# A four-stage image network on one core: softplus of the small pass earlier, gate later, sums moved, more banks in the small scans

## The reference

```
x = x + mamba_pyramid(gn(x))     # block 0, touched by the change
x = x + attention(gn(x))         # block 1, 8 heads of 32, 1024 tokens
x = x + dilated_depthwise(gn(x)) # block 2
x = x + attention_ln(gn(x))      # block 3
```

```
delta = softplus(dt(f) + dtb); dA = exp(delta * A); dBx = delta * B * f
h = h * dA + dBx               # along the tokens, 128 channels x 16 states
y = sum_n(h * C) + f * D; y = layernorm(y)
```

## Time and profile before

| | |
|---|---|
| median of 3 runs (range) | 5007.52 us (5001.81 to 5014.78) |
| profiled execution: time, span | 5008.71 us, 5007.0 us |
| mean granted clock of PE | 0.876 |
| busy: PE, DVE, ACT, POOL | 82%, 71%, 43%, 44% |
| from one sample's output to the next's | 617 to 624 us |
| of it in the 48 scans (sample 1) | 162 us |

### The profile page before, as it was taken

One profiled execution on the slowest core, in us unless ns is written; L12 is line 12 of the kernel. 1 busy time (PEld: TensorE's weight loads), 2 busy tenths in 40 slices (PEclk: granted clock), 3 DMA queues, 4 the chain that ended last, 5 costly groups with the idle time before them and its releaser, 6 DMA issues. The chain is left out here.

```text
span 5007.0 us, 46959 instructions
## 1 busy us (share of the span) xinstructions
PE 4130.5 (82%) x17450; PEld 1976.1 (39%) x17450; DVE 3559.5 (71%) x4904; ACT 2164.6 (43%) x2623; POOL 2205.8 (44%) x777
## 2 busy tenths in 40 slices
PE   5699976999769997699976999769896798967988
PEld 2254432444324443244433444334443344423443
DVE  6865787657776577765777757877678675786756
ACT  4334453335533355243552435524355242652525
POOL 4731546315464155540555505555056450564505
PEclk8799987999879997799977999779997799977999
DMA  1020200201002110021100210002200012001120
GB/s 39 0 60 1 51 9 0 60 16 36 9 0 60 22 31 9 1 60 28 24 9 9 52 36 16 9 9 52 48 4 9 21 40 51 1 9 26 27 51 10
DMA packets 62967, 125.92 MB, mean 25 GB/s; under 512 B 18825, under 2 KB 21001, under 8 KB 62482
## 3 DMA queue, kind: packets, MB, share of 16 engines
q1 hardware_dynamic: 62738, 122.91, 10.6%
HBM read 12.23 MB, written 8.39 MB: 4 GB/s over the span
## 5 line engine op out<-in xcount | busy, mean ns | idle before, releaser
L1039 DVE TENSOR_REDUCE mx<-PS 128x1 f32<-128x512 f32 x2048 | 1280.0, 684 | 418.2 <-PE PS L1407 416.9
L675 ACT ACTIVATE PT<-PS 128x1024 f32<-128x1024 f32 x1024 | 999.9, 1021 | 856.6 <-PE PS L1512 847.4
L430 POOL TENSOR_TENSOR piece<-PT 128x2048 f32<-128x2048 f32 x48 | 220.2, 4588 | 1890.5 <-ACT PT L675 1890.5
L1407 PE MATMUL PS<-KS,QS 96*128 96x512 f32 x2048 | 841.4, 470 | 66.8 <-DVE mx L1039 29.4
L430 POOL TENSOR_TENSOR piece<-piece,PT 128x2048 f32<-128x2048 f32 x192 | 880.1, 4584 | 16.4 <-ACT PT L675 1.5
L1512 PE MATMUL PS<-QS,KS 98*128 98x512 f32 x2048 | 670.4, 419 | 41.2 <-DMA QS<-nm 41.0
L410 POOL TENSOR_TENSOR work<-work,Crep 128x1024 f32<-128x1024 f32 x256 | 605.0, 2392 | 57.6 <-PE PS L1287 37.1
L1407 PEld LDWEIGHTS PS<-KS,QS 96*128 96x128 f32 x2048 | 374.5, 197 | 566.7 <-DVE mx L1039 401.3
L1460 PE MATMUL PS<-PT,Vt 128*32 128x512 f32 x4096 | 548.1, 607 | 26.5 <-DVE oT L1063 19.3
L1327 PE MATMUL PS<-dstk,sel 128*128 128x512 f32 (+1 forms) x640 | 292.5, 529 | 230.9 <-DVE work L924 93.7
L1512 PEld LDWEIGHTS PS<-QS,KS 98*128 98x128 f32 x2048 | 382.2, 197 | 247.2 <-ACT PT L675 110.8
(11 more groups left out here) (222 smaller groups left out, 5359.8 us busy)
## 6 DMA issues: line engine op xcount, KB each, us to landing
QS<-piece SPq DMA_DIRECT2D x384, 128.0 KB, 2.4
KS<-piece SPq DMA_DIRECT2D x384, 128.0 KB, 2.4
xin<-x SPq DMA_DIRECT2D x8, 1024.0 KB
out<-xr SPq DMA_DIRECT2D x8, 1024.0 KB, 4.0
W<-wpack SPq DMA_DIRECT2D x2, 1024.0 KB
QS<-nm SPq DMA_DIRECT2D x128, 8.0 KB, 1.9
W<-wpack SPq DMA_DIRECT2D x1, 576.0 KB
W<-wpack SPq DMA_DIRECT2D x2, 256.0 KB
```

The costliest lines, as they stand in the source:

```text
L430: pool.tensor_tensor(total, first, PT[:, i % PT_RING, :, :], ALU.add).then_inc(sum_pool.sem, 1)
L675: act.activation(PT[:, i % PT_RING, 2 * pr:2 * pr + 2, :], PS[:, 2 + 2 * pr:4 + 2 * pr, :], ACT.Exp, scale=SCALE).then_inc(p_sb.sem, 1)
L1039: dve.tensor_reduce(mx[:, at, cc:cc + 1], PS[:, row_slot(n, cc), :], AX.X, ALU.max).then_inc(r_max.sem, 1)
L1407: pe.matmul(PS[:, row_slot(n, cc), :], QS[0:kd, c, h, q * P:q * P + P], KS[0:kd, h, cc * N:cc * N + N], start=True, stop=True).then_inc(r_ ...
```

## The change

Six edits, all in block 0 but the last:

1. The small pass's softplus input (`coeff(2, 0, Wd)`) is computed earlier on PE, and ACT runs its softplus right after `head_of_input(0)`, ahead of the coefficient copies of pass 1.
2. The gate moves: its two halves go to banks 1 and 0, the first ahead of the scans, the second on PE after n = 1, and ACT applies Silu (two halves, both table loads) ahead of its work for n = 2.
3. The ring of C products gets eight slots (two of them in `xr`), and most sums go at 4q + 8 instead of 4q + 6.
4. The inputs of states 19 and 31 are made by DVE and no longer by ACT and POOL.
5. In the small scans u goes to banks 2 and 3 in turn and d to banks 4, 6, 5, 7 in turn; the waits follow.
6. In attention the head of the negative maximum is copied as soon as it is there, the rest by ACT's queue; at the first phase ACT issues both.

```
+POOL_INPUTS = (3, 7, 11, 15, 23, 27)
+STATES = 8
...
-        decay_of = lambda n: PS[:, 4 + 2 * (n % 2):6 + 2 * (n % 2), :].rearrange("p a n -> p (a n)")
+        decay_bank = lambda n: 4 + 2 * (n % 2) if n < 2 * SG else (4, 6, 5, 7)[n % 4]
...
+        input_bank = lambda n: 2 if n < 2 * SG else 2 + n % 2
...
+        hC_slot = lambda n: work[:, 6 + n % STATES, :] if n % STATES < 6 else xr[:, n % STATES - 6, :]
...
-                for ph in range(PHASES):
+                for ph in range(1, PHASES):
                     g, c = divmod(ph, NC)
-                    sp.wait_ge(*nm_rest(b, PHASES * a + ph + 1))
-                    for part in range(2):
-                        sp.dma_start(QS[96 + part:97 + part, c, GH * g:GH * g + GH, :].bitcast(F32),
-                                     nm[:, part, :].bitcast(F32)).then_inc(nm_in.sem, 16)
+                    sp.wait_ge(*nm_head(b, PHASES * a + ph + 1))
+                    sp.dma_start(QS[96:97, c, GH * g:GH * g + GH, :].bitcast(F32),
+                                 nm[:, 0, :].bitcast(F32)).then_inc(nm_in.sem, 16)
...
-                    if n >= 6:
-                        pool.wait_ge(*y_ps(b, (n - 6) // 4 + 1))
+                    if n >= STATES:
+                        pool.wait_ge(*y_ps(b, (n - STATES) // 4 + 1))
+                    if n == 6:
+                        pool.wait_ge(*xr_free(b, 16))
...
                 head_of_input(0)
-                coefficient(1, Brep, brep_ps, brep_sb, 2)
-                coefficient(1, Crep, crep_ps, crep_sb, 4)
-                act.wait_ge(*z_ps(b, 2))
-                act.activation(xg[:, 0, :], PS[:, 2:4, :].rearrange("p a n -> p (a n)"), ACT.Silu,
-                               bias=v("in_b", 1)).then_inc(z_sb.sem, 1)
-                act.preload_act_table_set("natural_log_exp_and_others")
                 magnitude(2)
                 decayed(2)
                 quadratic(2)
                 logarithm(2)
+                coefficient(1, Brep, brep_ps, brep_sb, 2)
+                coefficient(1, Crep, crep_ps, crep_sb, 4)
+                coefficient(2, Brep, brep_ps, brep_sb, 1)
                 head_of_step(1)
-                coefficient(2, Brep, brep_ps, brep_sb, 1)
...
+                def gate():
+
+                    act.wait_ge(*z_ps(b, 2))
+                    for c in range(NC):
+                        act.activation(xg[:, 0, c * N:c * N + N], PS[:, 1 - c, :], ACT.Silu,
+                                       bias=v("in_b", 1)).then_inc(z_sb.sem, 1)
+                    act.preload_act_table_set("natural_log_exp_and_others")
+
...
+                    if n == 2:
+                        gate()
...
+                def copy_part(ph, part):
+
+                    g, c = divmod(ph, NC)
+                    act.wait_ge(*(nm_head, nm_rest)[part](b, PHASES * a + ph + 1))
+                    act.dma_start(QS[96 + part:97 + part, c, GH * g:GH * g + GH, :].bitcast(F32),
+                                  nm[:, part, :].bitcast(F32)).then_inc(nm_in.sem, 16)
+
+                copy_part(0, 0)
+                copy_part(0, 1)
...
+                        if kt == TURN_AT and ph < PHASES - 1:
+                            copy_part(ph + 1, 1)
...
-                    src = PS[:, 2:4, :].rearrange("p a n -> p (a n)")[:, 0:w]
+                    src = PS[:, 2:4, :].rearrange("p a n -> p (a n)") if ps < 2 else PS[:, input_bank(n), 0:w]
...
                 coeff(0, 2, w_xb, brep_ps)
+                coeff(2, 0, Wd, pre_ps)
...
-                pe.wait_ge(*brep_sb(b, 2))
-                for c in range(NC):
-                    linear(2 + c, w_in, 1, xg, c, z_ps)
-                coeff(2, 0, Wd, pre_ps)
...
+                pe.wait_ge(*brep_sb(b, 3))
+                linear(1, w_in, 1, xg, 0, z_ps)
...
-                        slot = (2, 4 + 2 * (n % 2))[kind]
+                        slot = (input_bank(n), decay_bank(n))[kind]
...
+                        if kind == 0 and n > 2 * SG:
+                            pe.wait_ge(*dBx_sb(b, n - 1 - pool_inputs(n - 1)))
+                        elif kind == 0 and n >= 1 and not on_pool(n - 1):
                             pe.wait_ge(*dBx_sb(b, n - pool_inputs(n)))
                         if kind == 1 and n >= 2:
-                            pe.wait_ge(*scanned(b, scans(n - 2)))
+                            pe.wait_ge(*scanned(b, scans(n - 2 if n < 2 * SG + 2 else n - 4)))
...
+                    if n == 1:
+                        linear(0, w_in, 1, xg, 1, z_ps)
...
-    return 4 * q + (SUM_AFTER_NORM if q in (4, 8) else SUM_LATE)
+    return 4 * q + (SUM_LATE if q in (3, 6, 7) else SUM_AFTER_NORM)
...
-    return n % 4 == 3 and n < 2 * SG
+    return n in POOL_INPUTS
```

More of the change, by code:

```diff
@@ L186, in build @@
         u_of = lambda ps: yv[:, 2, :] if ps == 0 else dl_of(ps)
-        decay_of = lambda n: PS[:, 4 + 2 * (n % 2):6 + 2 * (n % 2), :].rearrange("p a n -> p (a n)")
+        decay_bank = lambda n: 4 + 2 * (n % 2) if n < 2 * SG else (4, 6, 5, 7)[n % 4]
+        decay_of = lambda n: (PS[:, decay_bank(n):decay_bank(n) + 2, :].rearrange("p a n -> p (a n)") if n < 2 * SG
+                              else PS[:, decay_bank(n), :])
+        input_bank = lambda n: 2 if n < 2 * SG else 2 + n % 2
         dBx_slot = lambda n: (work[:, 2, :], work[:, 3, :], yv[:, 2, :])[n % 3]
@@ L236, in build @@
         d_ps, u_ps = sig("d_ps", 48), sig("u_ps", 48)
-        dA_sb, dBx_sb = sig("dA_sb", 64), sig("dBx_sb", 40)
-        u_sb, dBx_pool = sig("u_sb", 8), sig("dBx_pool", 8)
+        dA_sb, dBx_sb = sig("dA_sb", 64), sig("dBx_sb", 3 * SG - len(POOL_INPUTS))
+        u_sb, dBx_pool = sig("u_sb", len(POOL_INPUTS)), sig("dBx_pool", len(POOL_INPUTS))
         scanned, hC_sb, y_ps = sig("scanned", 96), sig("hC_sb", 48), sig("y_ps", 12)
@@ L243, in build @@
         levels = sig("levels", 10)
-        z_ps, z_sb, gated = sig("z_ps", 2), sig("z_sb", 1), sig("gated", 1)
+        z_ps, z_sb, gated = sig("z_ps", 2), sig("z_sb", 2), sig("gated", 1)
         o_ps, x_new = sig("o_ps", 16), sig("x_new", 16)
@@ L394, in sample @@
                     ps, at = n // SG, PASS_AT[n // SG]
-                    if n >= 6:
-                        pool.wait_ge(*y_ps(b, (n - 6) // 4 + 1))
+                    if n >= STATES:
+                        pool.wait_ge(*y_ps(b, (n - STATES) // 4 + 1))
+                    if n == 6:
+                        pool.wait_ge(*xr_free(b, 16))
                     if n == 0:
                         pool.wait_ge(*crep_sb(b, 3))
-                    slot = work[:, 6 + n % 6, :]
+                    slot = hC_slot(n)
                     h = h_of(n)
@@ L983, in block0 @@
                 dve.wait_ge(*xr_free(b, 16))
-                dve.wait_ge(*z_sb(b, 1))
+                dve.wait_ge(*z_sb(b, 2))
                 dve.tensor_tensor(work[:, 11, :], y1, xg[:, 0, :], ALU.mult).then_inc(gated.sem, 1)
@@ L1279, in sum_states @@
                     pe.wait_ge(*hC_sb(b, 4 * q + 4))
+                    if q == 0 and c == 0:
+                        pe.wait_ge(*z_sb(b, 2))
                     if q == 4:
@@ L1284, in sum_states @@
                     for j in range(4):
-                        hc = work[:, 6 + (4 * q + j) % 6, :]
+                        hc = hC_slot(4 * q + j)
                         src = hc[:, c * N:c * N + N] if ps < 2 else hc[:, c * N:c * N + W3]
@@ L1308, in block0 @@
                 pe.wait_ge(*crep_sb(b, 3))
-                pe.wait_ge(*z_sb(b, 1))
                 for n in range(3 * SG):
@@ L1317, in block0 @@
                     for kind, (stk, done) in enumerate(((ustk, u_ps), (dstk, d_ps))):
-                        slot = (2, 4 + 2 * (n % 2))[kind]
+                        slot = (input_bank(n), decay_bank(n))[kind]
                         if kind == 0 and n >= 1 and on_pool(n - 1):
                             pe.wait_ge(*u_sb(b, pool_inputs(n)))
-                        if kind == 0 and n >= 1 and not on_pool(n - 1):
+                        if kind == 0 and n > 2 * SG:
+                            pe.wait_ge(*dBx_sb(b, n - 1 - pool_inputs(n - 1)))
+                        elif kind == 0 and n >= 1 and not on_pool(n - 1):
                             pe.wait_ge(*dBx_sb(b, n - pool_inputs(n)))
                         if kind == 1 and n >= 2:
-                            pe.wait_ge(*scanned(b, scans(n - 2)))
+                            pe.wait_ge(*scanned(b, scans(n - 2 if n < 2 * SG + 2 else n - 4)))
                         for c in range((w + N - 1) // N):
```

## The result

The kernel after takes 4807.5 us (median of 4 runs, 4803.94 to 4815.45) against 5008.69 us (5001.81 to 5014.78) before: ratio 0.9601, 95% interval 0.9583 to 0.9619. The profiled execution of after has a span of 4803.5 us and a mean granted clock of 0.905 (before 0.876).

The account below looks back on a forecast made before the run. The bound changes from stage to stage, with DVE setting the pace in the scans. Terms of 13.7 us a sample, taken as 13.2, give 8 x 13.2 + 28 = 134 off 5009: 4875 us, range 4812 to 4935.

Parts of the forecast that it names:

- Preparation: Preparation of block 0: the new order removes DVE's 6.77 us of idle time, a gain of 6.8 us a sample.
- Late gate: Gate's second half on PE before state 2's input: costs DVE 1.9 us a sample, with ACT's work hidden.
- Sums apart and eight slots: Large scans: shorter DVE stalls, gaining 1.8 us at states 8, 12, 16, 1.6 at 28, 0.3 at 24, a sample.
- States 19 and 31: Large scans: DVE gets 2 x 1.2 us, stalls shrink by about 2, 0.5 is charged: net -0.9 us a sample.
- Banks: Small scans: extra input and decay banks give PE one more state of lead, a gain of 6.0 us a sample.
- Copies of the maximum: Attention: earlier copies gain 22 us at the attentions' starts and 6 at the other 48 turns, 28 once.
- A: Rival, chance 0.22: DVE runs nearly without gaps, idle in the scans falls to 5 us a sample; 4814 us.
- B: Rival, chance 0.21: the large scans give nothing, with PE at the low clock; 4928 us.
- C: Rival, chance 0.04: slower, as sums directly before u cost 3.8 us a group against 1.26; 5061 us.
- D: Rival, chance 0.03: a table load in the scans costs more than its 1.28 us, scan 2 1.5 late; 4887 us.

Follow-up runs that it names:

- e3: The changed kernel with one input bank and two decay banks in the small scans, with the waits of before: 4845.69 us, ratio to before 0.9676.

## Why the prediction missed

**Preparation.** Right: 6.85 for 6.8. What I took as one thing is two: 5.5 for the gate's going, 1.4 for the early softplus. The first sample gained 9.55, 2.7 us more; in e3 it gained only 7.1 with the same code there, so part of that varies between executions.

**Late gate.** The cover of ACT's 3.8 us held, and a table load cost its 1.28. The stall was well sized for sample 1 (1.55 for 1.9, PE at the low clock as supposed), but that is the sample with the longest; the mean is 0.92. And even that is more than the cost, as a stall here goes with shorter ones behind it: 0.3 us in the kernel before, and nothing gained by the split gate in the kernel after.

**Sums apart and eight slots: the step that failed.** The mechanism was right and the term was mis-sized: 3.7 us a sample forecast, 8.75 measured on the kernel before and 7.1 taken away from the kernel after, 56 to 70 us and not 30. Four things are in it:

- In sample 1, states 8, 12, 16: 2.0 us for 1.8, state 28: 2.25 for 1.6, state 24: none for 0.3. These were sized well, the first of them partly by luck: I mixed no stall at the high clock with 1.4 at the low one. PE's first half sum took 1.60 us at state 8, between the two levels' 1.06 and 1.94, and u came in time; at states 12 and 16 it took the low clock's 1.94, and u was 0.66 and 0.93 late, not 1.4.
- The stalls at states 20 and 32 (1.27, 1.30, 0.59 and 0.36 at a step of the layer norm) I had put down to edit 4, less 0.5. With slots and sums alone they shrink from 3.5 to 0.6. That is 2.9 us a sample in the wrong term, and the 0.5 for "two pairs of sums in four states" was nothing.
- One multiplication of the layer norm in the large scans fell from 2.10 to 1.20 us (last section): 0.9 a sample, of which the forecast knew nothing. One in the small scans fell too, by 0.6 in the mean.
- I read one sample. Its large scans are 0.74 shorter than the mean in the trace of before and 0.52 longer in that of after: 1.26 a sample, 10 us, that no reading of sample 1 alone could give. At state 24, for one, DVE idles 0.82 us in sample 1 of before, but 3.40 in samples 2 and 3 and 1.64 in the mean.

Over all eight samples the stalls account for the step, from before to slots and sums together: 2.1 us at states 8, 12 and 16 (now 9, 13 and 17), 1.0 at state 20 with its step of the layer norm, 0.8 at 24, 2.2 at 28, 1.85 at 32, and the multiplication's 0.9: 8.9 for the measured 8.75.

**States 19 and 31.** Forecast -0.9, measured 1.5 lost in the large scans and 1.1 won in the small ones, -0.4: the right sign, half the size, and by other stalls than I named. The two kernels' times can't be told apart.

**Banks.** The 16 small scans gained 6.29 for 6.0, but the banks alone give 2.6 to 2.8. The rest is POOL's being earlier (slots and sums, 2.3 in the kernel before, the multiplication's 0.6 within that) and state 31 on DVE (1.1). These don't simply add: with banks and edit 4 in place, taking slots and sums away costs the small scans 0.3 only. So the 6.0 was right by luck. I had written all under the banks because I sized the stretch's stalls and not the edit.

**Copies of the maximum.** Right in sum: 28 for 28. At the attention's start that the earlier trace rows show the gain is 1.1 us (4.36 to 3.25), not 1.4; the other turns give the more.

**Rivals.** The time is nearest to A (4814), but by luck: A wants PE at the high clock where sums and states meet, and its first half sums there took 1.60, 1.94 and 1.94 us; 0, 0.66, 0.93 and 0.82 us of stall are left, and idle time in the scans of sample 1 fell to 9.7 us, not 5. The multiplication and the clock behind the scans, which A didn't have, help to make up for that. B, at the low clock, and C are out: C's mechanism is real, though, for the moved sums without the slots cost 29 us; it came by way of POOL's slots, not by PE's clock. D is out by the row. The range was too narrow below because I treated the stalls of a burst as independent of the ones that the same queue causes four states later; that this is what links states 12 and 16 to 20 and 32 is argued, while it is measured that the two edits bring those two from 3.5 to 0.6 us.

## What to carry to other kernels

Where two queues hold each other (PE frees POOL's slots, POOL feeds PE's sums), price the two edits that loosen them as one: alone they were worth +25 and -29 us here, together 89. Size an edit by the stalls whose releaser's own wait it removes, and ask that for every stall of the stretch, also those at the places that another edit of the same diff names. And take the mean over all repetitions of a stretch before reading one of them: sample 1 alone was off by 1.3 us of 6.4, and by 0.6 of 0.9 at the gate.

## What the runs showed of the hardware

**DVE and POOL slow each other where DVE reads two operands from SBUF.** The multiplication of the layer norm (both inputs from SBUF), 16 times in the kernel: first before (L887, min/median/max in ns), then after (L911):

```profile
L887 DVE TENSOR_TENSOR yv<-yv,xg x16: 1627/2102/2236, 171.6 to 4561.6; 128x1024 f32<-128x1024 f32 x16
```

```profile
L911 DVE TENSOR_TENSOR yv<-yv,xg x16: 1196/1200/1201, 159.7 to 4368.3; 128x1024 f32<-128x1024 f32 x16
```

Before, POOL's product runs when it starts; it had waited for PE's sum:

```profile
787.91 5.65 POOL L410 TENSOR_TENSOR work<-work,Crep 128x1024 f32<-128x1024 f32 x2 [3.81 <-PE PS L1287]
789.24 2.11 DVE L887 TENSOR_TENSOR yv<-yv,xg 128x1024 f32<-128x1024 f32 x1
```

After, DVE comes first and POOL's product, 2.38 us elsewhere, takes 3.19:

```profile
753.46 1.20 DVE L911 TENSOR_TENSOR yv<-yv,xg 128x1024 f32<-128x1024 f32 x1
...
753.68 3.19 POOL L417 TENSOR_TENSOR work<-work,Crep 128x1024 f32<-128x1024 f32 x1 [0.70 <-DVE work L948]
```

In all kernels with eight slots the median is 1.20 us, in those with six 1.73 to 2.11. Of the 16 in before, the eight in the large scans take 2.10 to 2.12 us and those in the small ones, beside a smaller product of POOL, 1.63 to 1.65 (six) or 2.2 (two): the mean is 1.94, so about 16 x 0.74 = 12 us of DVE's time are saved here. The Trainium skill (SBUF — State Buffer, SBUF: two separate sides) says that such a DVE operation and a POOL operation take their common port in turn, the later one being held until the first has ended; the two pairs of rows agree, 0.9 us lost by DVE in the one and 0.8 by POOL in the other.

**The clock behind the scans.** In the 10 us from the next input's DMA (the group norm behind block 0) the granted clock is 0.83 before, in all 8 samples, and 1.00 after, in all 8; sample 1 of each, the columns as in the earlier trace rows:

```profile
885.20:895.50 10.30, 8.88 (x41) 6.97 (x42) 2.97 (x9) 1.71 (x3) 0.00 (x0) 0.83 0.35 110
```

```profile
839.38:849.60 10.22, 8.80 (x44) 6.03 (x45) 3.02 (x10) 2.82 (x4) 0.00 (x0) 1.00 0.34 111
```

The code there is the same. It is worth some 1.2 us a sample from that DMA to the first scores (2.25 less the 1.09 that the copies give), 9 us that no term of the forecast had. With eight slots alone, where the copies are as before, the six samples at 1.00 are 1.2 us shorter than the same samples of before, and the two at 0.83 are not. The kernels with a shorter small pass often have 1.00 (eight slots alone and banks alone: 6 of 8 samples), before, moved sums alone and the early preparation alone 0.83 in all 8. But slots and sums together have 0.83 in 6 of 8 samples, the split gate with states 19 and 31 on POOL in 5 of 8, and the kernel after with one input bank in all 8, each with a shorter small pass than eight slots alone, so length isn't the rule; what decides it stays open.
